# Attention plus mixture of experts on eight cores: the first expert's second matrix is fetched and cast at other places, and the attention's steps get another order

## The reference

```python
x = layernorm(x + attn(x))        # x: 8 x 2048 x 1024
x = layernorm(x + ffn(x))

# attn: q, k, v = silu(causal depthwise conv(x @ W.T)); 4 heads of 256; beta, gamma, mix = sigmoid(x @ W.T)
# delta rule in chunks:  T = inverse of a lower triangular matrix of k and beta, u = T v, w = T k
for each chunk:
    u_new = u - w @ S
    o     = q @ S + masked(q k^T) @ u_new
    S     = S + k^T u_new
o = (1 - mix) * o + mix * ema(v, gamma);  o = rmsnorm(o) @ Wo.T

# ffn: expert choice, 8 experts, each takes its 512 best rows
probs = softmax(x @ choice_w.T);  G, I = top_k(probs^T, 512)
h     = silu(x[I] @ w1[e])        # 1024 -> 2048
out[I] += G * (h @ w2[e])         # 2048 -> 1024
```

## Time and profile before

| | us |
|---|---|
| median of 3 runs | 1136.87 (1131.53 to 1214.22) |
| the profiled execution | 1132.01 |
| its span, slowest core (2) | 1130.5 |
| spans of all cores | 1112.6 to 1130.5 |
| TensorE busy | 972.2 (86%) |
| VectorE / ScalarE / GpSimd busy | 506.8 / 517.8 / 311.1 |

### The profile page before, as it was taken

The page is one execution under the profiler, slowest core; times in us unless marked ns, Lnnn a source line. Parts: engine busy times, 40 slices in busy tenths (PEclk is TensorE's granted clock), DMA queues, the critical chain, the costliest instruction groups (busy, mean ns, idle before and its releaser), DMA issues.

```text
span 1130.5 us, 20991 instructions; the slowest of 8 cores (1112.6 to 1130.5 us)
## 1 busy us (share of the span) xinstructions
PE 972.2 (86%) x6351; PEld 524.8 (46%) x6471; DVE 506.8 (45%) x1190; ACT 517.8 (46%) x875; POOL 311.1 (28%) x417
## 2 busy tenths in 40 slices
PE   3989979899989999989802889999999999999991
PEld 1445645555555556555402434444444444444440
DVE  3557646667666667786657232021202020101372
ACT  2556656666666666688841302212121313131271
POOL 1123334434543342222101213130312112131044
PEclk9999999999999999999955989999999999999996
DMA  9986878976797776237781999999998989894794
GB/s 249 170 166 133 156 171 147 186 181 165 137 188 162 169 153 148 113 113 248 250 316 42 254 283 183 244 180 242 186 231 154 237 147 252 145 293 118 259 363 176
DMA packets 48603, 217.90 MB, mean 193 GB/s; under 512 B 6148, under 2 KB 6148, under 8 KB 39152
## 3 DMA queue, kind: packets, MB, share of 16 engines
q0 software_dynamic: 23728, 101.40, 50.4%
q1 hardware_dynamic: 24768, 115.15, 29.6%
HBM read 219.50 MB, written 67.11 MB: 254 GB/s over the span
## 4 chain that ended last, share of the span: by engine, by line
PE 62%; DMA 19%; issue 6%; DVE 5%; ACT 3%; POOL 3%; SPq 1%; DVEq 0%; POOLq 0%; ACTq 0%
PE ps L1413 17%; PE ps L1390 15%; PE ps L516 9%; DMA AR<-w 9%; DMA w<-AR 6%; PE ps L561 3%; PE ps L1026 3%; DMA AR<-accd 2%; PE ps L593 2%; PE ps L796 1%; PE ps L786 1%; DVE AR L1232 1%; DMA AR<-hsT 1%; PE ps L1336 1%; PE ps L937 1%
## 5 line engine op out<-in xcount | busy, mean ns | idle before, releaser
L1390 PE MATMUL ps<-AR 128*128 128x512 bf16 x1000 | 227.2, 383 | 13.1 <-ACT AR L1496 11.5
L1413 PE MATMUL ps<-AR 128*128 128x512 bf16 x969 | 216.6, 379 | 1.2
L516 PE MATMUL ps<-AR 128*128 128x512 bf16 x753 | 181.4, 381 | 1.0 <-issue 0.2
L1390 PEld LDWEIGHTS ps<-AR 128*128 128x128 bf16 x1024 | 93.5, 98 | 122.0 <-issue 16.9
L1522 ACT ACTIVATE AR<-ps 128x512 bf16<-128x512 f32 x128 | 76.1, 597 | 160.3 <-PE ps L1390 159.1
L1413 PEld LDWEIGHTS ps<-AR 128*128 128x128 bf16 x992 | 95.8, 98 | 111.2
L1496 ACT ACTIVATE AR<-ps 128x1024 bf16<-128x1024 bf16 x32 | 32.6, 1024 | 202.2 <-PE ps L1336 202.2
L516 PEld LDWEIGHTS ps<-AR 128*128 128x128 bf16 x768 | 71.3, 98 | 72.7 <-issue 2.7
L1462 DVE TENSOR_SCALAR AR<-ps,gcol 128x512 f32<-128x512 f32 x48 | 33.8, 746 | 140.8 <-PE ps L1413 140.8
L550 DVE CAST AR<-ps 128x512 bf16<-128x512 f32 x96 | 66.0, 688 | 57.9 <-PE ps L516 57.7
L1563 POOL DMA_INDIRECT accd<-AR,idxc x24 | 38.1, 1586 | 152.9 <-DVE AR L1462 104.4
(11 more groups left out here) (184 smaller groups left out, 1514.9 us busy)
## 6 DMA issues: line engine op xcount, KB each, us to landing
AR<-w POOLq DMA_DIRECT2D x56, 512.0 KB, 8.0
w<-AR SPq DMA_DIRECT2D x56, 512.0 KB, 4.5
AR<-w POOLq DMA_DIRECT2D x28, 1024.0 KB, 20.2
AR<-w SPq DMA_DIRECT2D x28, 1024.0 KB, 16.5
AR<-w SPq DMA_DIRECT2D x8, 2048.0 KB, 17.0
AR<-hs SPq DMA_DIRECT2D x16, 512.0 KB, 5.1
accd<-AR SPq DMA_DIRECT2D x16, 512.0 KB, 3.4
AR<-accd SPq DMA_DIRECT2D x16, 512.0 KB, 10.0
```

What stands on the lines that cost most here:

```text
L516: mm = T.matmul(ps[:, 0:512], w[:, kk, 128 * (i % 2):128 * (i % 2 + 1)], g.hs_fm[b][:, 512 * kk:512 * (kk + 1)], start=(kk == 0), stop=(kk ...
L1390: mm = T.matmul(ps[:, 0:512], w1[:, kk, 128 * (m % 4):128 * (m % 4 + 1)], xe[:, KTOP * kk:KTOP * (kk + 1)], start=(kk == 0), stop=(kk == 7))
L1413: mm = T.matmul(pss[nh][:, 0:512], g.h_fm[kk][:, 128 * tm:128 * (tm + 1)], w2[:, kk % 4, 512 * nh:512 * (nh + 1)], start=(kk == 0), stop=( ...
```

## The change

It has two parts. First, the second matrix of expert 0. Loads 4 and 5 go out ahead of SyncE's wait for gather 0, loads 6 and 7 stay behind it. ScalarE casts x = 0..5, all before the transposed rows. GpSimd casts x = 6 and 7, after it has issued the first-matrix quarters 4 and 5 and ahead of gather 1. VectorE casts none, and the function `dve_first` and its semaphore go. TensorE waits for ScalarE's cast for quarters 0 and 1 of the second matrix and for GpSimd's for 2 and 3. Second, the table `PLACE` has other positions throughout; stage offsets are the same. GpSimd's resulting order in the attention is unchanged. On the other engines steps move by a few places. In TensorE's order of a unit, these neighbours change, among others:

- before: `o 3, em 0, t 13, P 0, k 0`; after: `o 3, em 0, t 13, k 0, P 0`
- before: `t 1, o 0, k 1, t 2, C 0`; after: `t 1, o 0, t 2, C 0, k 1`
- before: `t 6, C 2, ot 0, t 7, k 2, C 3`; after: `ot 0, t 6, C 2, t 7, k 2, ot 1, C 3`
- before: `P 4, u 2, ot 1, t 9, P 5, em 2, o 2, t 10`; after: `P 4, t 9, em 2, u 2, P 5, o 2, t 10`
- before: `u 3, ss, t 12, o 3`; after: `u 3, t 12, ss, o 3`

On VectorE, before: `k 2, t 8, P 4, u 2, t 9`; after: `t 8, k 2, u 2, t 9, t 10, P 4`.

```diff
 PLACE = {
...
-    ('t', 12): (-1, 0.906, 0.843, 0.866, None),
+    ('t', 12): (-1, 0.849, 0.843, 0.823, None),
...
-    ('k', 0): (0, 0.057, 0.024, None, None),
+    ('k', 0): (0, 0.013, 0.012, None, None),
...
-    ('k', 1): (0, 0.244, 0.189, None, None),
+    ('k', 1): (0, 0.280, 0.270, None, None),
...
-    ('u', 2): (0, 0.631, 0.640, 0.430, None),
+    ('u', 2): (0, 0.760, 0.627, 0.399, None),
...
@@ pe_moe
                     if kk % 4 == 0 and e == 0:
-                        T.wait_ge(g.v_e0.sem, g.v_e0.at(Q))
+                        s = g.a_e0 if Q < 2 else g.p_e0
+                        T.wait_ge(s.sem, s.at(4 + Q))
@@ dve_moe
                 dve_onehot(g, V, e + 2, t)
-                if e == 0 and t % 4 == 3:
-                    dve_first(g, V, t // 4)
@@
+def first_place(g, x):
+    return g.w1r[x] if x < 4 else g.w2r[x - 4]
...
+def pool_first(g, P, x):
+    P.wait_ge(g.d_e0[stage(x)].sem, g.d_e0[stage(x)].at(x))
+    P.tensor_copy(out=first_place(g, x), in_=g.ste[stage(x)]).then_inc(g.p_e0.sem, g.p_e0.up(x))
@@ act_moe
-    for q in range(4):
-        act_first(g, A, q)
+    for x in range(6):
+        act_first(g, A, x)
@@ pool_moe
     load_w1(g, P, 5)
+    for x in (6, 7):
+        pool_first(g, P, x)
     pool_gather(g, P, 1)
@@ sp_stage
-    if 3 <= x < 7:
+    if x >= 3:
         Y.wait_ge(g.a_e0.sem, g.a_e0.at(x - 3))
-    elif x == 7:
-        Y.wait_ge(g.v_e0.sem, g.v_e0.at(0))
@@ sp_moe
-    for x in range(4):
+    for x in range(6):
         sp_stage(g, Y, x)
     for c in range(4):
         Y.wait_ge(g.d_ga[c].sem, g.d_ga[c].at(0))
-    for x in range(4, 8):
+    for x in (6, 7):
         sp_stage(g, Y, x)
```

More of the change, by code:

```diff
@@ L85 @@
     ("a_x1b", 1), ("a_x1f", 1), ("pe_xp", 1), ("a_xf", 1), ("pe_lg", 1), ("v_lg", 1), ("a_exp", 1), ("v_r2", 1),
-    ("pe_r", 1), ("v_oh", 1), ("pe_ls", 1), ("v_ix", 1), ("v_rr", 1), ("a_e0", 1), ("v_e0", 1),
+    ("pe_r", 1), ("v_oh", 1), ("pe_ls", 1), ("v_ix", 1), ("v_rr", 1), ("a_e0", 1), ("p_e0", 1),
     ("pe_gx", 1), ("a_gx", 1), ("pe_f1", 1), ("a_f1", 1), ("pe_f2", 1), ("v_f2", 1), ("a_fin", 1),
@@ L302 @@
 PLACE = {
[L303 to L335, removed]
@@ L336 @@
-    ('t', 10): (-1, 0.794, 0.704, 0.707, None),
-    ('t', 11): (-1, 0.818, 0.775, 0.741, None),
-    ('ef',): (-1, None, None, None, 0.355),
-    ('t', 12): (-1, 0.906, 0.843, 0.866, None),
-    ('t', 13): (-1, 0.967, 1.012, 0.889, None),
-    ('em', 0): (0, -0.047, None, -0.061, None),
-    ('k', 0): (0, 0.057, 0.024, None, None),
-    ('u', 0): (0, 0.143, 0.107, None, None),
-    ('o', 0): (0, 0.228, 0.227, 0.068, None),
-    ('k', 1): (0, 0.244, 0.189, None, None),
-    ('em', 1): (0, 0.271, None, 0.271, None),
@@ L347 @@
-    ('u', 1): (0, 0.281, 0.259, 0.348, None),
-    ('o', 1): (0, 0.362, 0.413, 0.319, None),
-    ('k', 2): (0, 0.467, 0.534, None, None),
-    ('u', 2): (0, 0.631, 0.640, 0.430, None),
[L351 to L357, removed]
@@ L358 @@
-    ('ot', 0): (1, 0.439, None, 0.449, None),
-    ('ot', 1): (1, 0.697, None, 0.652, None),
+    ('G',): (-2, -0.419, -0.373, -0.482, None),
+    ('P', 0): (-2, 0.029, 0.020, None, None),
+    ('P', 1): (-2, 0.163, 0.173, None, None),
+    ('GT',): (-2, 0.186, 0.193, None, None),
+    ('C', 0): (-2, 0.263, None, 0.236, None),
+    ('P', 2): (-2, 0.344, 0.343, None, None),
+    ('C', 1): (-2, 0.362, None, 0.397, None),
+    ('P', 3): (-2, 0.403, 0.403, None, None),
+    ('C', 2): (-2, 0.451, None, 0.466, None),
@@ new lines @@
+    ('C', 3): (-2, 0.660, None, 0.594, None),
+    ('P', 4): (-2, 0.704, 0.718, None, None),
+    ('P', 5): (-2, 0.775, 0.727, None, None),
+    ('V', 0): (-2, 0.793, None, 0.776, None),
+    ('V', 1): (-2, 0.823, None, 0.778, None),
+    ('sq',): (-2, None, None, 0.607, None),
+    ('ss',): (-1, -0.113, -0.054, None, -0.018),
+    ('gb',): (-1, 0.044, None, 0.044, None),
+    ('t', 0): (-1, 0.089, 0.054, 0.096, 0.096),
+    ('kt',): (-1, 0.093, None, 0.111, None),
+    ('vt',): (-1, 0.141, None, 0.119, None),
@@ new lines @@
+    ('mt', 0): (-1, None, 0.218, None, None),
+    ('t', 1): (-1, 0.169, 0.169, 0.169, 0.169),
+    ('t', 2): (-1, 0.246, 0.216, 0.194, 0.173),
+    ('t', 3): (-1, 0.310, 0.294, 0.264, 0.253),
+    ('mt', 1): (-1, None, 0.326, None, None),
+    ('t', 4): (-1, 0.352, 0.352, 0.346, 0.352),
+    ('t', 5): (-1, 0.390, 0.390, 0.390, 0.390),
+    ('t', 6): (-1, 0.450, 0.420, 0.404, 0.464),
+    ('t', 7): (-1, 0.461, 0.507, 0.500, 0.514),
+    ('mt', 2): (-1, None, 0.465, None, None),
+    ('mt', 3): (-1, None, 0.533, None, None),
@@ new lines @@
+    ('t', 8): (-1, 0.663, 0.592, 0.605, 0.660),
+    ('t', 9): (-1, 0.720, 0.629, 0.703, None),
+    ('t', 10): (-1, 0.783, 0.704, 0.705, None),
+    ('t', 11): (-1, 0.819, 0.791, 0.789, None),
+    ('t', 12): (-1, 0.849, 0.843, 0.823, None),
+    ('ef',): (-1, None, None, None, 0.366),
+    ('t', 13): (-1, 0.998, 1.012, 0.865, None),
+    ('em', 0): (0, -0.002, None, -0.091, None),
+    ('k', 0): (0, 0.013, 0.012, None, None),
+    ('u', 0): (0, 0.079, 0.052, None, None),
+    ('o', 0): (0, 0.184, 0.301, 0.159, None),
@@ new lines @@
+    ('k', 1): (0, 0.280, 0.270, None, None),
+    ('em', 1): (0, 0.306, None, 0.273, None),
+    ('u', 1): (0, 0.345, 0.318, 0.300, None),
+    ('o', 1): (0, 0.378, 0.388, 0.363, None),
+    ('k', 2): (0, 0.575, 0.624, None, None),
+    ('em', 2): (0, 0.752, None, 0.624, None),
+    ('u', 2): (0, 0.760, 0.627, 0.399, None),
+    ('o', 2): (0, 0.778, 0.725, 0.633, None),
+    ('k', 3): (0, 0.796, 0.769, None, None),
+    ('em', 3): (0, 0.804, None, 0.720, None),
+    ('u', 3): (0, 0.848, 0.802, 0.839, None),
@@ L360 @@
+    ('o', 3): (0, 0.979, 0.970, 0.835, None),
+    ('rms',): (1, None, None, -0.049, 0.056),
+    ('ot', 0): (1, 0.421, None, 0.442, None),
+    ('ot', 1): (1, 0.651, None, 0.577, None),
 }
@@ L1417, in pe_moe @@
                 pe_gx(g, T, e + 1, tm)
[L1420 to L1424, removed]
 def dve_moe(g, V):
@@ L1498, in act_gx, with act_first @@
                  func=AF.Copy).then_inc(g.a_gx.sem, g.a_gx.up(e, c))
-def act_first(g, A, q):
-    if q == 0:
+def first_place(g, x):
+    return g.w1r[x] if x < 4 else g.w2r[x - 4]
+def act_first(g, A, x):
+    if x == 0:
         A.wait_ge(g.pe_V.sem, g.pe_V.at(NU - 1, 1))
-    A.wait_ge(g.d_e0[stage(q)].sem, g.d_e0[stage(q)].at(q))
-    A.activation(out=g.w1r[q], in_=g.ste[stage(q)], func=AF.Copy).then_inc(g.a_e0.sem, g.a_e0.up(q))
+    A.wait_ge(g.d_e0[stage(x)].sem, g.d_e0[stage(x)].at(x))
+    A.activation(out=first_place(g, x), in_=g.ste[stage(x)], func=AF.Copy).then_inc(g.a_e0.sem, g.a_e0.up(x))
+def pool_first(g, P, x):
+    P.wait_ge(g.d_e0[stage(x)].sem, g.d_e0[stage(x)].at(x))
+    P.tensor_copy(out=first_place(g, x), in_=g.ste[stage(x)]).then_inc(g.p_e0.sem, g.p_e0.up(x))
 def act_moe(g, A):
```

## The result

| | before | after |
|---|---|---|
| median | 1136.26 (1131.53 to 1214.22, 7 runs) | 1128.98 (1127.04 to 1199.42, 7 runs) |
| ratio | | 0.9947, 95% interval 0.9925 to 0.9968 |
| profiled execution, its span | 1132.01, 1130.5 (core 2) | 1128.56, 1126.6 (core 4) |
| first expert, its start to the next one's, mean of 8 cores | 67.6 | 63.4 |
| second expert | 58.97 | 58.97 on cores 4 to 7, 59.85 on 0 to 3 |

A forecast was written before the change was run, and what follows sets the result against it. TensorE, busy 86% of the span, and its waits were taken as the bound. Slowest core 1130.5 - 9.4 (first expert) - 2.5 (table) = 1118.6; 1.5 around the span gives 1120.1, 2 toward the median gives 1122; range 1108 to 1138.

The forecast's parts named there:

- Part 1: First expert: loads 4 and 5 ahead of the gathers; ScalarE's two added casts, 7.2 us, end by 611 and cost nothing.
- part 2: First expert: GpSimd casts quarters 6 and 7 in time, VectorE is freed; gather 1 costs 0 to 1 us.
- rival D: First expert: GpSimd's casts are stretched to 8.3 us beside VectorE, 2 to 4 us back, 1125; chance 0.06.
- E: First expert: load 7 still lands at 666.9 and the second matrix stops 12 us for weights, 1133; chance 0.04.
- The price of the cast, 4.15: First expert: each GpSimd cast taken as four times L750's 1.037 us, 4.15 us, with bounds 2.29 and 8.3.
- about 61: First expert on core 6, whose first group runs at half clock: needs about 61 us instead of 68.5, gains 7.4.
- 59.1: First expert on core 2: would need 30.95 + 28.2 = 59.1 us, a gain of 11.1.
- Part 3: Attention table: swapped neighbours save 0.84 us and lose 0.29, 0.17 and 0.20: -0.18 a unit, -2.5 us in 14 units.
- rival C: Attention table: the new waits come and the old one stays, 9.9 us lost, 1134; chance 0.11.
- Rival G: Attention: VectorE stands still at `u 2` with two ready steps behind it, 1.37 us a unit, 1142; chance 0.09.
- Nothing else on it is late: the one-hots take 0.2 us each and the groups come every 1.76 us.: First expert: VectorE, rid of 4 x 2.29 us of casts and its DMA waits, delays nothing; TensorE is next late.
- The slowest core gains 9.4 us: First expert: core 2 falls to 1119.4, core 6 becomes slowest at 1121.1, so the slowest core gains 9.4 us.

The follow-up runs named there:

- after_again: The changed kernel run once more, unchanged, on the second chip, beside the kernel before: median 1129.68, ratio 0.9958.
- pool_pieces_again: Repeat on the third chip of the changed kernel with each GpSimd cast made in eight pieces of 512 columns: median 1124.84, 0.9930 of the kernel before.
- k0_back: The changed kernel with quarters 6 and 7 cast by ScalarE, and `P 0` ahead of `k 0` again: median 1132.37, 0.9998 of before, unit 27.6 us.
- table_only: The kernel before with the changed table and the old first expert: median 1132.51, 0.9990 of before.
- k1_only: The kernel before with one number changed, TensorE's position of `k 1` from 0.244 to 0.265: median 1134.21, 0.9988 of before, unit 27.0 us.
- k1_u1: The kernel before with `k 1` and `u 1` both moved later in the table: median 1137.28, 1.0025 of before, unit 26.9 us.
- act_casts: The changed kernel with quarters 6 and 7 cast by ScalarE after groups 10 and 14, none by GpSimd: median 1132.92, 0.9954 of before; repeat 1124.87, 0.9927.
- after_third: The changed kernel run again, unchanged, on the third chip, beside the kernel before: median 1129.45, ratio 0.9976.

## Why the prediction was wrong, step by step

**What held.** Part 1: ScalarE's two casts took 3.62 us each and ended 7.8 us before ScalarE was wanted. In part 2 the loads came early enough, on core 4 for casts that ended at 642.9 and 649.1, against 644.8 and 653.1 in my sum for core 2; gather 1 was issued at 649.28 there, TensorE waited neither for a quarter nor for gather 1, and rivals D and E did not come. The price of the cast, 4.15, was 0.55 too high and on no path. The sum's "about 61" for a first expert that begins at half clock is what the cores show without the hold (61.2), and its 59.1 for one at full clock is 59.16, seen on one core each of after_again, pool_pieces_again and k0_back.

**Part 3, right in its total, with luck in the terms.** Forecast -2.5 us in all, and the undisturbed cores of table_only show -2.8, uncertain by about 0.9. The -0.18 a unit meets the -0.21 between the commonest intervals, 26.83 and 26.62, but the intervals differ. Nine of the fifteen between the 16 casts at L750 are free of stalls on some core; there the shortest over the eight cores fell by 0.34 us on the mean, while the second and the last, where the three stages fill and empty, grew from 28.93 to 31.11 and from 28.68 to 30.22. The forecast had neither. Terms of it can be looked for in one unit, core 2, for the earlier trace rows:

```profile
269.83 0.27 PE L917 MATMUL ps<-AR 128*128 128x256 bf16 x1
270.14 0.38 PE L786 MATMUL ps<-AR 128*128 128x128 bf16 x4
...
271.94 0.28 PE L869 MATMUL ps<-c_s,AR 128*128 128x128 bf16 x2
272.33 0.38 PE L890 MATMUL ps<-AR 128*128 128x256 bf16 x2
...
278.77 0.27 PE L946 MATMUL ps<-AR 128*128 128x256 bf16 x1
279.17 0.38 PE L786 MATMUL ps<-AR 128*128 128x128 bf16 x4
...
286.46 0.39 PE L786 MATMUL ps<-AR 128*128 128x128 bf16 x4
...
287.69 0.38 PE L796 MATMUL ps<-AR 128*128 128x128 bf16 x4
...
291.40 0.27 PE L869 MATMUL ps<-c_s,AR 128*128 128x128 bf16 x2
291.51 0.27 PE L917 MATMUL ps<-AR 128*128 128x256 bf16 x1
```

The last pair shows the pace: 0.11 us from L869 to its neighbour. `k 0` at 272.33 comes 0.39 after L869, so 0.28 late; I had 0.29. `t 12` at 270.14 is 0.20 late in the same way (0.31 after a predecessor of 0.11); I had 0.17. `t 7` at 287.69 comes 1.23 after `t 6`, where `t 6` and `C 2` take 1.09 (0.22, and the 0.87 of a step C): 0.14 late, I had 0.20. And `t 2`, which now stands behind `o 0` and has lost the cover of k 1's wait, is 0.29 late at 279.17; I had put that at nothing. The view of waits shows such short ones only in part, yet these four eat 0.91 of the 1.07 us that the old waits held in the rows (0.84 and 0.23). That the same saving can turn into a loss, which was rival C, is what k1_only, k1_u1 and k0_back show: +0.15, +0.02 and +1.0 us a unit for tables that were each to remove a wait. Rival G did not happen: `V 0` (L593) waits 0.8 us in two pieces over the whole attention, where G wanted 1.37 in every unit.

**The step that failed: "Nothing else on it is late: the one-hots take 0.2 us each and the groups come every 1.76 us."** That priced VectorE as freed. Instead the GpSimd cast of 3.60 us holds VectorE's one-hots (L1312) and its addition L1322, which take their data from SBUF. On core 4 it is 2.35 us at 643.28 (the list was due 1.78 after the one at 639.15) and 1.47 us for the half-clock group behind it, 3.8 of the 4.2 us that lie between this core's 65.19 and core 5's 61.02, where no list had to wait. In the mean of cores it is 2.0 to 2.3 us (63.2 to 63.5 against 61.2), and it differs by core because it depends on whether a cast falls on a one-hot that is wanted. My own rival D had the pair of engines right and the direction wrong: it looked for a GpSimd cast stretched by VectorE, and took the even length of L750 as evidence against it. If GpSimd goes first, its length says nothing; VectorE's does. The trace of before had such a row, a VectorE L735 that began beside GpSimd's L526 (256.75 to 257.81, 128 x 512, both reading SBUF) and took 1.15 us where the median of this line is 0.68, as the timeline of core 2 shows:

```profile
257.21 1.15 DVE L735 SCALAR_TENSOR_TENSOR AR<-AR 128x512 f32<-128x512 f32 x1
```

```profile
256.75 1.06 POOL L526 TENSOR_TENSOR AR<-c_s,small_s 128x512 bf16<-128x512 bf16 x1
```

It had regular ones too. VectorE's L823, which has both inputs in SBUF, begins inside GpSimd's L990 in 13 of its 16 instances of before and ends 0.28 us after it each time; with the new table it begins 0.14 us earlier in L990, in 12 of 13 cases, and takes that much longer (view of the line, core 2 of before, then of after):

```profile
L823 DVE TENSOR_TENSOR AR<-AR,c_s x16: 402/579/584, 46.1 to 477.4; 128x512 bf16<-128x512 bf16 x16
```

```profile
L823 DVE TENSOR_TENSOR AR<-AR,c_s x16: 399/722/727, 46.7 to 468.8; 128x512 bf16<-128x512 bf16 x16
```

But not all that reads SBUF is held. L831, with one input in SBUF and one in PSUM, takes its usual 0.68 us inside GpSimd's L1773 of 2.86 us (before, core 2):

```profile
269.64 0.68 DVE L831 SCALAR_TENSOR_TENSOR AR<-AR,ps 128x512 bf16<-128x512 bf16 x1
```

```profile
268.41 2.86 POOL L1773 TENSOR_SCALAR AR<-AR,small_s 128x1024 bf16<-128x1024 bf16 x1
```

The rule stands in the Trainium skill in full, on the page SBUF — State Buffer, section "SBUF: two separate sides", which I had not used: whichever of a GpSimd instruction and a VectorE instruction in a two-port mode, or with two SBUF inputs (this only against a GpSimd instruction that reads SBUF), starts first has the shared pair of ports for its whole length, and the other one is blocked. The traces agree: 3.05 us for a two-input addition of 0.17, up to 3.65 us for a one-hot of 0.25, nothing for the copy from PSUM. No run here shows in which mode the one-hots ran. By that rule two casts of 3.6 us are two holds of up to 3.6 us each on a list that is due every 1.78 us.

**A second term, the slowest core.** "The slowest core gains 9.4 us" was made from cores 2 and 6 of one execution, whose first experts took 70.19 and 68.50. The mean of the eight cores was 67.6, and without the hold it falls to 61.2 in two profiles: 6.4 us. Against that mean the 9.4 overstates by 3.0. The hold takes 2.0 to 2.3 more. And from the profiled execution to the median I added 2 where the median of before lay 4.9 above; this alone makes 2.9 of the 14.9. The three together are 8.1 of the 8.9 us by which forecast and measured difference differ. Of these act_casts isolates the hold; the other two are arithmetic. My explanation of the 3.0, that the slowest core of one execution owes part of its long first expert to bad luck there, is only partly borne out: with VectorE's casts the slowest core has 70.2, 69.1, 69.5 and 67.8 in four profiles, always above the mean of 67 to 68, and in the four with one whole GpSimd cast for each quarter 65.2 to 65.6 where the mean is 63 to 64. Some 1 us was this execution's own; for the rest, the slowest core loses more than the mean to either wait, which fits the 3 us that the hold costs it where the mean has 2.0 to 2.3.

**The chip of the first profile.** Its cores 0 to 3 ran the second expert 0.9 us slower than the others, but that isn't the missing gain: after_again and after_third, without it, have 0.9958 and 0.9976.

The range of 1108 to 1138 held the median, and so did the 0.86 for a change within 2%.

## What to carry to other kernels

Before work goes to GpSimd, ask which VectorE instructions are queued while it runs and who waits for them: it is cheap in its own row and dear in another's, so cut it into short instructions or give it to ScalarE. In a chain ordered by hand, a step moved behind cover hands its wait to the chain's next step: price the whole chain, by the gaps between starts too, since the view of waits named few of those under 0.3 us that made up the table's cost. And forecast a gain from all cores and more than one execution, not from the slowest core of a single one.
